# Query and key parts copied straight into the stack, and GpSimd held until the mixed heads are normalised

## The reference

```python
# x: (32, 375, 64), 4 heads of width 16, 4 query experts per head
sx = einsum('bsh,ndh->bnsd', x, hl_w) + hl_b
q = einsum('bnsd,neod->bneso', sx, wq)          # 16 queries per token: 4 heads x 4 experts
k = einsum('bnsd,nod->bnso', sx, wk)            # 4 keys per token
v = einsum('bnsd,nod->bnso', sx, wv)
scores = einsum('bnesd,bntd->bnest', q, k) * 16 ** 0.5 + causal
qkv = einsum('bnest,bntd->bnesd', softmax(scores), v)
gs = softmax(gates of the four experts)
mixed = einsum('bnsed,bnse->bnsd', qkv, gs)
hn = layernorm(mixed + first heads)             # the norm of the mixed heads
hx = layernorm(two small layers of hn + hn)
out = x + hx * softmax(hx @ fgate_w.T)
```

## Time and profile before

| | |
|---|---|
| median of three runs | 3397.48 us (3371.49 to 3411.12) |
| profiled execution | 3390.36 us, span 3388.6 us |
| PE busy | 3081.6 us (91%) |
| PEld busy | 2193.7 us (65%) |
| DVE busy | 2615.6 us (77%) |
| ACT busy | 1817.5 us (54%) |
| POOL busy | 1301.8 us (38%) |
| mean granted TensorE clock | 0.920 |

### The profile page before, as it was taken

How to read it: one execution, slowest core, us unless ns; L and a number is a source line. 1 busy time by engine, 2 the same in 40 slices (tenths; PEclk the granted TensorE clock), 3 DMA queues, 4 the chain that set the end, 5 groups by cost and what they waited for, 6 DMA issues and landing times.

```text
span 3388.6 us, 81043 instructions
## 1 busy us (share of the span) xinstructions
PE 3081.6 (91%) x24964; PEld 2193.7 (65%) x24964; DVE 2615.6 (77%) x7699; ACT 1817.5 (54%) x4484; POOL 1301.8 (38%) x1368
## 2 busy tenths in 40 slices
PE   0699999999999899998999998999999999999995
PEld 0588888888888634444777776666666666666663
DVE  4788888888888578886888865788777777778773
ACT  0355555555555445554766643555555555555552
POOL 1443444434344144441000022445445444444432
PEclk9999999999999989997888867999889989989996
DMA  4100000000000000000000013443333333333420
GB/s 140 35 22 22 14 21 14 21 20 15 21 14 8 1 1 0 0 0 1 1 0 0 0 28 58 71 66 64 59 59 59 58 59 60 70 57 63 68 36 4
DMA packets 74280, 110.98 MB, mean 33 GB/s; under 512 B 20105, under 2 KB 65481, under 8 KB 73577
## 3 DMA queue, kind: packets, MB, share of 16 engines
q1 hardware_dynamic: 72936, 106.85, 16.9%
q10 hardware_dynamic: 1024, 0.39, 0.0%
HBM read 76.01 MB, written 30.82 MB: 32 GB/s over the span
## 4 chain that ended last, share of the span: by engine, by line
PE 25%; issue 9%; POOL 6%; DMA 6%; DVE 5%; SPq 2%; ACT 1%; POOLq 0%; DVEq 0%; ACTq 0%
DMA qe_K<-query_key_parts 4%; PE psum L2329 3%; PE psum L1660 3%; PE psum L2315 2%; PE psum L2343 2%; POOL qe_root L3032 2%; PE psum L2302 2%; DMA query_key_parts<-qe_parts 2%; PE psum L2366 2%; PE psum L1689 2%; PE psum L1677 1%; SPq L2221 1%; PE psum L1731 1%; SPq L2223 1%; POOL qe_parts L3014 1%
## 5 line engine op out<-in xcount | busy, mean ns | idle before, releaser
L2782 DVE TENSOR_REDUCE qe_top<-psum 125x1 f32<-125x375 f32 (+2 forms) x896 | 500.8, 596 | 238.1 <-PE psum L2302 235.7
L2589 ACT ACTIVATE qe_E<-psum 125x375 f32<-125x375 f32 (+1 forms) x896 | 459.0, 531 | 285.1 <-PE psum L2302 261.0
L2302 PE MATMUL psum<-bconst 125*125 125x125 bf16 (+2 forms) x1792 | 491.3, 274 | 0.0
L625 PE MATMUL psum<-Q,K 96*125 96x125 f32 (+3 forms) x2304 | 404.5, 311 | 0.5 <-ACT E L836 0.4
L2315 PE MATMUL psum<-qe_K,qe_Q 96*125 96x375 bf16 (+2 forms) x1536 | 332.0, 300 | 59.4 <-DMA qe_K<-query_key_parts 32.3
L625 PEld LDWEIGHTS psum<-Q,K 96*125 96x125 f32 (+1 forms) x2304 | 334.3, 189 | 24.5 <-issue 1.2
L2329 PE MATMUL psum<-qe_Q,qe_K 97*125 97x375 bf16 (+2 forms) x1536 | 336.8, 299 | 2.4 <-ACT qe_E L2589 2.0
L1175 POOL TENSOR_TENSOR Q<-rot 64x375 f32<-64x375 f32 (+1 forms) x256 | 305.7, 1213 | 73.4 <-DVE rot L976 61.4
L836 ACT ACTIVATE E<-psum 125x500 f32<-125x500 f32 x384 | 226.2, 589 | 172.7 <-PE psum L645 169.5
L2315 PEld LDWEIGHTS psum<-qe_K,qe_Q 96*125 96x125 bf16 x1536 | 182.4, 148 | 167.1 <-DVE qe_top L2782 71.6
L2302 PEld LDWEIGHTS psum<-bconst 125*125 125x125 bf16 x1792 | 266.4, 149 | 9.8 <-issue 6.9
(11 more groups left out here) (341 smaller groups left out, 7199.7 us busy)
## 6 DMA issues: line engine op xcount, KB each, us to landing
qe_Q<-query_key_parts SPq DMA_DIRECT2D x192, 187.5 KB, 6.2
query_key_parts<-qe_parts SPq DMA_DIRECT2D x32, 843.8 KB, 3.6
s_row<-scores SPq DMA_DIRECT2D x32, 366.2 KB
qe_K<-query_key_parts SPq DMA_DIRECT2D x192, 46.9 KB, 6.6
x_tokens<-x SPq DMA_DIRECT2D x32, 187.5 KB
x_chunks<-x SPq DMA_DIRECT2D x4, 750.0 KB
E<-x SPq DMA_DIRECT2D x4, 750.0 KB
out<-qe_hout SPq DMA_DIRECT2D x32, 93.8 KB
```

Of the source, the lines that this page charges most:

```text
L625: nc.tensor.matmul(out[:, first * TP:(first + n) * TP].rearrange("p (o q) -> p o q", o=n), t.K[0:rows(h), par, h, jt * TP:(jt + 1) * TP], ...
L2302: return nc.tensor.matmul(out, B("ident_b")[0:TP, 0:TP], rhs, start=False, stop=True, skip_group_check=True)
L2589: nc.scalar.activation(E[:, e % 2, a:a + width], bank[0:TP, 4 + n % 2, 0:width], ACT.Exp).then_inc(e_done, 1)
L2782: nc.vector.tensor_reduce(dst, src, AX, ALU.max).then_inc(m_read, 1)
```

## The change

Four edits, all for the last stage:

- The columns of the projection weights (`w_heads`) are put in another order: for the queries the partition of a projection is now (dimension, head, half of the experts), for the keys (half, dimension, head). With it a row group of the stack can be read from `parts` in SBUF as one plain copy.
- The DRAM tensor `query_key_parts`, its store and the wait for it are gone. The twelve DMAs read `parts` in SBUF. The six that need only part 0 (`Q` of groups 0, 1 and 3, `K` of groups 0, 2 and 5) are issued when `hi_done` is there and the slot is free, the other six (`K` of 1, 3, 4, `Q` of 2, 4, 5) after `parts_done`.
- ScalarE's `first_part(b, ., 0)`, which overwrites `parts`, waits for `stacked`, all twelve copies of example `b-1`, where it waited for the store.
- GpSimd gets `yield_port`: behind `take_root(bs[5], ., 0)` it waits for `fx_ready` of that example, and only then goes on with `leave_rest`, `other_parts` and the rest.

```diff
--- before.py
+++ after.py
@@ -209,14 +209,14 @@
     wide[D, :, DH2] = 1.0
     k.add("w_sx_wide", wide.reshape(96, 128))
     k.add("w_sxT", np.concatenate([l["hl_w"].reshape(D, D), l["hl_b"].reshape(D, 1)], 1))
-    heads = z(D, 4, HE, 2, DH2)
+    queries, keys, values = z(D, 2, DH2, HE, 2), z(D, 1, 2, DH2, HE), z(D, 1, HE, 2, DH2)
     for n in range(HE):
         rows = slice(n * DH2, (n + 1) * DH2)
         for e in range(EE):
-            heads[rows, e % 2, n, e // 2] = l["wq"][n, e].T
-        heads[rows, 2, n, 0] = l["wk"][n].T
-        heads[rows, 3, n, 0] = l["wv"][n].T
-    k.add("w_heads", heads.reshape(D, 4, 128))
+            queries[rows, e % 2, :, n, e // 2] = l["wq"][n, e].T
+        keys[rows, 0, 0, :, n] = l["wk"][n].T
+        values[rows, 0, n, 0] = l["wv"][n].T
+    k.add("w_heads", np.concatenate([v.reshape(D, -1, 128) for v in (queries, keys, values)], 1))
     gw = z(128, EE, HE * EE)
     for n in range(HE):
         for e in range(EE):
@@ -2176,7 +2176,7 @@
         r1, foT, hout = sb("r1", [D, S]), sb("foT", [D, S]), sb("hout", [TP, 3, NT * D])
 
         folded, set_up, p_ready, v_ready, nz_ready, nz_done, v_kept = map(sem, ("folded", "set_up", "p", "v", "nz", "nz_done", "v_kept"))
-        hi_done, full_done, parts_done, parts_stored, stacked = map(sem, ("hi", "full", "parts", "parts_stored", "stacked"))
+        hi_done, full_done, parts_done, stacked = map(sem, ("hi", "full", "parts", "stacked"))
         m_ready, m_read, neg_ready, neg_turned, maxT_kept = map(sem, ("m", "m_read", "neg", "neg_turned", "maxT"))
         max_stacked = sem("max_stacked")
         e_ready, e_done, v_done, c_kept, c_masked = map(sem, ("e", "e_done", "v_done", "c_kept", "c_masked"))
@@ -2206,21 +2206,21 @@
             return min(value, most) if isinstance(value, int) else value
 
         def sync(sp):
-            rows_of = qk_dram.rearrange("(a d) p i s -> p d a i s", d=DH2)
-            keys_of = qk_dram.rearrange("(h a d) p i s -> a p i d h s", a=2, d=DH2)
-
             def stack(b, slot):
 
                 wait(sp, e_ready, (b - 2) * NU)
                 wait(sp, stacked, b * 32 * len(q_parts))
-                sp.wait_ge(parts_done, (b + 1) * NP)
-                sp.dma_start(qk_dram, parts[:]).then_inc(parts_stored, 16)
-                sp.wait_ge(parts_stored, (b + 1) * 16)
-                for g, (qp, kp) in enumerate(zip(q_parts, k_parts)):
-                    rows = slice(g * DH2, (g + 1) * DH2)
-                    sp.dma_start(Q[rows, slot].rearrange("d (a i) s -> d a i s", i=2), rows_of[qp, :, :, 0:2]
-                                 ).then_inc(stacked, 16)
-                    sp.dma_start(K[rows, slot], keys_of[0, kp, 2]).then_inc(stacked, 16)
+                sp.wait_ge(hi_done, (b + 1) * NP)
+                for first in (True, False):
+                    for g, (qp, kp) in enumerate(zip(q_parts, k_parts)):
+                        rows = slice(g * DH2, (g + 1) * DH2)
+                        if (qp == 0) == first:
+                            sp.dma_start(Q[rows, slot].rearrange("d q s -> d (q s)"), parts[:, qp, 0:2, :]).then_inc(stacked, 16)
+                        if (kp == 0) == first:
+                            sp.dma_start(K[rows, slot].rearrange("d h s -> d (h s)"),
+                                         parts[0:DH2 * HE, kp, 2, :]).then_inc(stacked, 16)
+                    if first:
+                        sp.wait_ge(parts_done, (b + 1) * NP)
 
             def store(b, slot):
                 sp.wait_ge(h_ready, (b + 1) * 16)
@@ -2562,7 +2562,7 @@
             def first_part(b, slot, i):
                 act.wait_ge(p_ready, b * NP + i + 1)
                 if i == 0:
-                    wait(act, parts_stored, b * 16)
+                    wait(act, stacked, b * 32 * len(q_parts))
                 nc.scalar.copy(parts[:, 0, i, :], bank[:, in_bank(b, i), 0:S]).then_inc(hi_done, 1)
 
             def whole(b, slot, i):
@@ -3033,6 +3033,9 @@
                 nc.gpsimd.tensor_tensor(rooted[:], root[:].rearrange("p (a o) -> p a o", o=1).to_broadcast((TP, NT * HE, DH2)),
                                         gamma[:, i], ALU.mult).then_inc(root_done, 1)
 
+            def yield_port(b):
+                pool.wait_ge(fx_ready, b + 1)
+
             def step(r, par):
                 on, bs = [alive(r - i, nb) for i in range(LAGS + 1)], [r - i for i in range(LAGS + 1)]
                 s = [(par - i) % 3 for i in range(LAGS + 1)]
@@ -3040,6 +3043,7 @@
                     mask_context(bs[4], s[4], 0)
                 if on[5]:
                     take_root(bs[5], s[5], 0)
+                    yield_port(bs[5])
                 if on[1]:
                     leave_rest(bs[1], s[1], 1)
                     other_parts(bs[1], s[1], 0)
...
```

More of the change, by code:

```diff
@@ L2113, in slices, with query_experts @@
         return tensor, scalar, vector, gpsimd
-def query_experts(k, ctx, qk_dram, out):
+def query_experts(k, ctx, out):
     nc, nb, F, B, W, bank = k.nc, k.nb, k.F, k.B, k.W, k.bank
@@ L3080, in one, with tower @@
     return h[:, bass.ds(b, 1), :].rearrange("p o f -> p (o f)")
-def tower(nc, nb, x, fpack, bpack, wpack, packs, s_dram, qk_dram, out):
+def tower(nc, nb, x, fpack, bpack, wpack, packs, s_dram, out):
     with ExitStack() as ctx:
@@ L3093, in tower @@
         with nc.cleanup_on_exit(), ExitStack() as c:
-            query_experts(k, c, qk_dram, out)
+            query_experts(k, c, out)
 def kernel(**inputs):
@@ L3111 @@
     out = nc.dram_tensor("out", (nb, S, D), F32, kind="ExternalOutput").ap()
-    qk_dram = nc.dram_tensor("query_key_parts", (128, 3, 3, S), BF16).ap()
     s_dram = nc.dram_tensor("scores", (nb * CI, TP), F32).ap()
-    tower(nc, nb, *args, (f, b, w), s_dram, qk_dram, out)
+    tower(nc, nb, *args, (f, b, w), s_dram, out)
     r = run_bass_kernel_spmd(nc, [arrays], core_ids=[0])
```

## The result

The changed kernel takes 3411.22 us (median of 20 runs, from 3397.32), the kernel before 3385.13 (median of 20, 3366.74 to 3411.12): ratio **1.0071, interval [1.0047, 1.0094]**. One of the 20 executions took 8222.98 us at a granted clock of 1.00, the other 19 at most 3430.17; the ratio leaves it out, no trace of it was kept and its cause stays open. So the change makes the kernel 0.7% slower, some 24 us, where I forecast 3510 and slower by over 1%. The new wait came as forecast, the slow clock that I expected behind it mostly did not: the result lies between my rivals B and C.

What follows compares the result with a forecast made beforehand. TensorE, 91% busy, was taken as the bound. Seven rounds of each of three kinds + 81, rounds ahead of the loop + 34, the last + 6: + 121 on 3390.4 gives 3510 us, range 3350 to 3570.

Steps and rivals of the forecast that it cites:

- B: Rival, chance 0.16: TensorE's new mid-round wait of 2.75 us comes but the clock holds, 3372 us.
- C: The prediction's own case, chance 0.60: new mid-round wait plus slow clock, 3510 us, own range 3430 to 3570.
- Part 1: Start of the round: the store goes, 843.8 KB out and one landing, 3.8 us off the chain into TensorE.
- part 2: SyncE: six of twelve copies move ahead, waiting for hi_done, and fit before the parts are ready at no cost.
- Part 3: Six late copies at 126 GB/s land 8.6 us after the parts (18.4 before); TensorE's waits for the keys become 0.
- A: Rival, chance 0.20: copies inside SBUF are fast, about 210 GB/s, so no new wait, 3290 us.
- D: Rival, chance 0.04: copies inside SBUF slower than 126 GB/s, each us later + 31, to 3600 us.
- Part 4: Mid-round: first_part waits for all twelve copies; TensorE idles 2.75 us a round, + 5.4 for slow clock, together 8.1.
- the lengths above: Round starts before the change: waits of 1.8 us or more had a slow stretch behind them, costing 5.4 us.
- Part 5: GpSimd yields, VectorE's fx steps end sooner: TensorE's 0.76 us wait ahead of turning fx goes; GpSimd waits some 0.9.
- no change within 1%: Outcome of the whole kernel within about 1% (34 us): the rest of B, chance 0.14.
- slower by more: Outcome of the whole kernel slower by more than about 1% (34 us): C and D, chance 0.63.

Runs made afterwards that it cites:

- split version: Changed kernel with the twelve copies counted on two semaphores, so first_part waits for the six early ones alone: 3275.48 us, ratio 0.9656 to the kernel before.

## Why the prediction was wrong, point by point

**Part 1, the store, and part 2, six copies early: right.** SyncE now waits for the parts (276.1 us, 31 times), with the early six issued long before.

**Part 3, the landing: right, to 0.1 us by luck.** Forecast 8.6 after the parts; the median of 31 is 8.5. My own terms give 8.8 (14.5 less 5.7), not 8.6, and they leave out that an issue takes longer here, 0.60 for 0.43: in the trace the six issues take 3.9 us and the last copy lands some 4.6 behind the last issue. The rate from the reads (126 GB/s) did carry over to copies inside SBUF: 124 with all queues busy. Rivals A and D fall by the landing alone, and so does B's condition, a landing under 7.7. At the 104 GB/s that the Trainium skill ("SBUF — State Buffer", Door 1) measured for partitions 0 to 15 the landing would have been at 9.8, as an estimate; the trace has 8.5.

**Part 4, `first_part`: right in mechanism and in the idle time, wrong in the slow clock.** ScalarE waits 4.2 us each time (forecast about 4), TensorE stands 2.0 to 2.3 (forecast 2.3), and a round without a slow stretch takes 37.2 to 37.4 (36.0 - 0.76 - 0.5 + 2.75 = 37.5 was the forecast, and rival B's round). The step that failed is "by the lengths above that is the size that brought the slow clock: + 5.4". I had that price from waits at the start of a round and applied it in the middle because the waits were as long. There the slow stretch was of 0, 3 or 7 us and cost 0, 1.4 or 2.7 (rounds of 37.3, 38.7 and 40.0), 1.3 in the mean of the 14 rounds without a jump in the loop. The runs with longer waits at either place show that the price goes with the place; why it does, they leave open.

**Part 5, the yield: right on VectorE, wrong on the sum.** The steps of `fx` are at 0.36. The 0.76 wasn't there to gain: without the yield, TensorE hardly waits for `fx` in the changed kernel. I had added up a gain and a new wait that hide each other. My price for GpSimd (0.9, hidden) held where nothing else is late (0.94 in the split version); in the changed kernel it stands 2.1 to 4.2 us, since VectorE has `fx` ready 2.0 to 4.0 us behind `rooted` there and 0.8 in the split version, and the parts are ready no later for it than without the yield (22.6 us behind `rooted` against 22.7, in rounds without a jump).

**The sum.** Forecast + 121, measured + 12.9 on the stage:

| | forecast | measured |
|---|---|---|
| 7 rounds with a jump | + 35 | 47.8 against 43.6: + 29 |
| 14 rounds without | + 46 | 38.6 against 39.6: - 14 |
| 7 rounds ahead of the loop | + 34 | 273.8 in all against 266.7: + 7 |
| first and last rounds | + 6 | - 10 |

The jump rounds were forecast at 48.6 and are 47.8: there the stretch behind the jump was long in either case, so the wrong price hardly entered. It entered 21 times elsewhere: 14 x (42.9 - 38.6) = 60 and 300.3 - 273.8 = 26, together 86 of the 108 us missed. The last row, 16 us, I haven't taken apart.

**The chances.** The measured 3411 lies in the range (3350 to 3570), above B's 3372 and below C's own 3430. As an outcome it is "no change within 1%", to which I had given 0.14, where "slower by more" had 0.63. What I listed as proof of B, "4 us and the clock at 1.00", came in some rounds and its opposite in others; I had no case between them, though the earlier trace rows and the rounds ahead of the loop had already shown waits that went both ways. The sentence that every wait of 1.8 us or more brought a slow stretch was true of the start of a round, where all of them stood.

## What to carry to other kernels

When a buffer's guard is moved from one transfer to another, ask which bytes the next writer really overwrites, and count those transfers alone: here one shared semaphore cost 4.1% and turned a gain of 3.4% into a loss of 0.7%. Price an idle gap of TensorE by gaps at the same place in the round, never by gaps of the same length elsewhere, and carry the range from nothing to the full price where the place is new. Judge a small saving only with the wait that follows it: the same yield was worth - 0.6%, 0 and + 1.2% in three surroundings.

## What the runs showed of the hardware

- The same idle time of TensorE has different prices in one round. Behind gaps of 3.3 to 5.4 us at the start of a round it ran at 1.2 GHz for 14 us, behind gaps of 4.3 to 5.0 in its middle for 3 to 7, behind gaps of 1.9 to 2.3 there for 0, 3 or 7. At the start of a round gaps of 1.2 us and more brought slow stretches of 10 to 14 in the kernel before with the yield, and gaps of 0.74 to 0.82 did so in four rounds (one of the kernel before, three of it without its loop), though most of that length did not. In every version without added products the longer of the two lengths at a place (7 or 14) came where the clock had fallen before TensorE went on, the shorter (3 or 10) where it fell after.
- TensorE can be busy all the while and stay at 1.2 GHz: behind the waits at the start of a round it was busy 9.4 and 9.6 of 10 us at a clock of 0.50.
- A jump back in this loop costs TensorE 3.1 to 4.1 us of waiting for its instructions, and with the slow clock behind it 8.5 us (split version). In the loop some landings of the store came 1.6 to 2.1 us later than the usual 3.5, without it none did.
- Copies inside SBUF that write 16 partitions each moved at the rate of the reads from DRAM, 124 and 126 GB/s with all queues busy. Their issue on SyncE takes 0.60 us each (median), where that of the reads took 0.43: with twelve in a round, 7.2 us of the queue.
- An elementwise step of VectorE on 192 columns takes 0.36 us alone and up to 1.11 beside GpSimd's operations on float32 tiles (0.72 in the mean of the changed kernel without the yield).
